# The combine phase in five parts, with all loads of both sums issued in the expert phase into buffers over the first layer's weights

## What is computed

```python
raw_gate = softmax(einsum('btd,de->bte', x, gate))
_, topk_idx = top_k(raw_gate, 3)
mask = one_hot(topk_idx, 16).sum(axis=2)
gate_topk = mask * raw_gate
gate_topk = gate_topk / maximum(sum(abs(gate_topk)), 1e-12)
hidden = relu(einsum('btd,edh->bteh', x, W1) + b1)
expert_out = einsum('bteh,ehd->bted', hidden, W2) + b2
x = layernorm(x + einsum('bte,bted->btd', gate_topk, expert_out))   # eps = 1e-5
```

## Time and profile before

| | us |
|---|---|
| median of 3 runs (lowest, highest) | 1821.72 (1820.7, 1823.14) |
| the profiled execution, own time | 1823.23 |
| its span in the trace | 1821.1 |
| PE busy in the span | 1678.5 (92%) |
| DVE busy | 1392.2 (76%) |
| POOL busy | 1225.5 (67%) |
| ACT busy | 731.6 (40%) |

### The profile page before, as it was taken

The page is one execution under the profiler, slowest core; times in us unless marked ns, Lnnn a source line. Parts: engine busy times, 40 slices in busy tenths (PEclk is TensorE's granted clock), DMA queues, the critical chain, the costliest instruction groups (busy, mean ns, idle before and its releaser), DMA issues. The chain is left out here.

```text
span 1821.1 us, 34011 instructions
## 1 busy us (share of the span) xinstructions
PE 1678.5 (92%) x9489; PEld 1260.4 (69%) x9490; DVE 1392.2 (76%) x3247; ACT 731.6 (40%) x1556; POOL 1225.5 (67%) x1051
## 2 busy tenths in 40 slices
PE   4689999999999999999999999999659999999990
PEld 3566667766666667666676666665339999999980
DVE  3568888888888888998888898887775665656655
ACT  2234454445444444445544444454352222222223
POOL 3257778777887777687876788665017777777764
PEclk9789999999999999999999999999859999999995
DMA  9976456755666777646686565541964444444448
GB/s 308 342 197 174 135 175 201 198 140 163 187 164 179 219 207 203 181 146 183 204 248 178 163 180 166 154 140 50 324 206 70 75 71 71 72 73 74 72 63 282
DMA packets 185395, 302.10 MB, mean 166 GB/s; under 512 B 23616, under 2 KB 82752, under 8 KB 185136
## 3 DMA queue, kind: packets, MB, share of 16 engines
q1 hardware_dynamic: 161888, 269.20, 49.9%
q0 software_dynamic: 21312, 30.02, 10.6%
q10 hardware_dynamic: 2064, 1.31, 0.3%
HBM read 188.67 MB, written 111.54 MB: 165 GB/s over the span
## 5 line engine op out<-in xcount | busy, mean ns | idle before, releaser
L814 ACT ACTIVATE prob<-b_ps 128x512 f32<-128x512 f32 (+3 forms) x768 | 354.6, 489 | 357.2 <-PE b_ps L613 261.1
L540 POOL TENSOR_TENSOR acc<-acc,prob 128x1024 f32<-128x1024 f32 (+1 forms) x188 | 348.3, 1853 | 6.2 <-POOL acc L540 5.2
L612 PE MATMUL b_ps<-q,k 128*128 128x512 f32 (+3 forms) x768 | 294.8, 388 | 4.9 <-ACT prob L814 3.0
L511 POOL TENSOR_TENSOR roped<-rot 128x512 f32<-128x512 f32 x128 | 174.8, 1366 | 166.6 <-DVE rot L959 165.8
L605 PE MATMUL a_ps<-k,q 128*128 128x512 f32 (+3 forms) x768 | 266.1, 383 | 19.7 <-DMA k<-scratch_hilo 9.0
L939 DVE CUSTOM_DVE_ANT_0 masked<-a_ps,causal 128x256 bf16<-128x256 f32 (+3 forms) x512 | 246.1, 496 | 45.3 <-PE a_ps L605 37.8
L695 PE MATMUL y_ps<-prob,v_sb 128*64 128x512 f32 (+3 forms) x1536 | 272.9, 490 | 0.0
L613 PE MATMUL b_ps<-q,k 65*128 65x512 f32 (+3 forms) x768 | 264.4, 348 | 0.0
L1555 POOL DMA_INDIRECT scratch_sum<-y,dst_i x111 | 184.9, 1665 | 96.0 <-ACT y L1627 95.1
L1004 DVE RECIPROCAL inv<-inv 128x128 f32<-128x128 f32 x252 | 229.1, 931 | 2.3
L516 POOL TENSOR_TENSOR lo<-roped,hi 128x512 fp32r<-128x512 f32 x128 | 176.1, 1376 | 81.1 <-ACT hi L827 81.1
(11 more groups left out here) (266 smaller groups left out, 2405.2 us busy)
## 6 DMA issues: line engine op xcount, KB each, us to landing
q<-scratch_hilo SPq DMA_DIRECT2D x192, 256.0 KB, 4.6
k<-scratch_hilo SPq DMA_DIRECT2D x192, 256.0 KB, 5.2
scratch_hilo<-hi SPq DMA_DIRECT2D x64, 512.0 KB, 4.0
scratch_hilo<-lo SPq DMA_DIRECT2D x64, 512.0 KB, 4.7
w_sb<-scratch_wsplit SPq DMA_DIRECT2D x32, 512.0 KB, 3.7
w<-in_L_ffn_W_dram SPq DMA_DIRECT2D x32, 512.0 KB, 9.6
wv_sb<-scratch_wsplit SPq DMA_DIRECT2D x16, 512.0 KB, 7.2
xT<-scratch_xsplit SPq DMA_DIRECT2D x6, 1024.0 KB, 7.6
```

What stands on the lines that cost most here:

```text
L540: nc.gpsimd.tensor_tensor(sums, old, probs(q), ALU.add).then_inc(m["sum_p"], 1)
L612: nc.tensor.matmul(out, k1[s][:, h, js], q1[s][:, h, qs], start=True, stop=False, skip_group_check=True)
L814: nc.scalar.activation(probs(q)[:, h, :], b_ps[:, h, 0:w], ACT.Exp).then_inc(exp_done[h], 1)
```

## The change

1. SP now issues all 16 loads inside the expert phase. Three loads of `sum1` go out when its last scatter has landed (L1542 of the changed kernel), then, behind the landing of the last scatter to `sum0`, the other 13 in turn (L1551, L1552). The combine phase's SP stream has only the stores left.
2. `got0` and `got1` are no longer buffers of the combine phase. They are laid over `w1` (`gathered_sums`), and the combine phase is moved inside the context that holds the weights. Since the loads overwrite `w1`, SP also waits for DVE's last copy out of it.
3. The parts of the layernorm are five: groups 0-1, 2-3, 4-5, 6, 7. DVE now takes the moments of one more group ahead of `finish` in the first three parts, and finishes the last two parts at the end. ACT takes roots 2 and 3 together, and root 4 between the tiles of part 2.
4. The means and variances (`mv`) and the chain's middle value (`near_ps`) lie in PSUM, and no instruction of `finish` has two inputs in SBUF any more; one small copy in each part (L1844) brings the variances to SBUF for ACT. The chain still has six instructions.
5. ACT normalizes 27 tiles, DVE the last 5.

```diff
-PART = 2
-LAST_PART = TILES - LOAD * PART
+PARTS = ((0, 2), (2, 4), (4, 6), (6, 7), (7, 8))
+AHEAD_LOADS = 3
...
+def gathered_sums(S):
+    places = S["w1"][:].rearrange("p e k h -> p (e k h)")
+    got1, got0 = places[:, 0:TILES * D], places[:, TILES * D:TILES * D + 2 * TB * D]
+    return tuple(t.rearrange("p (t d) -> p t d", d=D) for t in (got0, got1))
...
             sums = dram["sum1"].rearrange("(t p) d -> p t d", p=P)
             sp.wait_ge(ys_st[1], scattered(1))
-            sp.dma_start(S["x1b"][:, 0:LOAD, :], sums[:, 0:LOAD, :]).then_inc(S["both_in"][0], 16)
+            for g in range(AHEAD_LOADS):
+                rows = slice(LOAD * g, LOAD * (g + 1))
+                sp.dma_start(S["x1b"][:, rows, :], sums[:, rows, :]).then_inc(S["both_in"][g], 16)
+            sp.wait_ge(m["m_w1"], done(USED_TILES - 1))
+            sp.wait_ge(ys_st[0], scattered(0))
+            got0, got1 = gathered_sums(S)
+            even = dram["sum0"].rearrange("(t p) d -> p t d", p=P)
+            for g in range(LOADS):
+                rows = slice(LOAD * g, LOAD * (g + 1))
+                if g >= AHEAD_LOADS:
+                    place = S["x1b"][:, rows, :] if g < LOADS // 2 else got0[:, LOAD * g - 2 * TB:LOAD * (g + 1) - 2 * TB, :]
+                    sp.dma_start(place, sums[:, rows, :]).then_inc(S["both_in"][g], 16)
+                sp.dma_start(got1[:, rows, :], even[:, rows, :]).then_inc(S["both_in"][g], 16)
...
-        got0 = sb("got0", [P, HALF_TILES, D], F32)
-        got1 = sb("got1", [P, TILES, D], F32)
+        got0, got1 = gathered_sums(S)
...
-        mv = sb("mv2", [P, TILES, 2], F32)
-        r = sb("r2", [P, 5, TILES], F32)
+        small = ctx.enter_context(nc.psum_tensor("small2", [P, 512], F32))
+        mv = small[:, 0:2 * TILES].rearrange("p (t a) -> p t a", a=2)
+        near_ps = small[:, 2 * TILES:3 * TILES]
+        r = sb("r2", [P, 6, TILES], F32)
+        inverse, scales, shifts, _, variance, root_sb = (r[:, i, :] for i in range(6))
+        ACT_TILES = TILES - 5
...
-            for g in range(LOADS):
-                if g:
-                    sp.dma_start(sums_of(g), sums[1][:, rows(g), :]).then_inc(S["both_in"][g], 16)
-                sp.dma_start(got1[:, rows(g), :], sums[0][:, rows(g), :]).then_inc(S["both_in"][g], 16)
...
+            root(0)
+            normalize(0, 0, 8)
+            root(1)
+            normalize(1, 8, 16)
+            root(2)
+            root(3)
+            normalize(2, 16, 20)
+            root(4)
+            normalize(2, 20, 24)
+            normalize(3, 24, ACT_TILES)
...
-                link(V.tensor_tensor(a, first, first, ALU.mult))
-                link(V.scalar_tensor_tensor(out=root, in0=mv[:, tiles_of(h), 1], scalar=EPS, in1=a, op0=ALU.add,
+                link(V.scalar_tensor_tensor(out=near_ps[:, ts], in0=mv[:, ts, 1], scalar=EPS, in1=inverse[:, ts], op0=ALU.add,
                                             op1=ALU.mult))
...
+            moments(0)
+            moments(1)
+            moments(2)
+            finish(0)
+            moments(3)
+            moments(4)
+            finish(1)
+            moments(5)
+            moments(6)
+            finish(2)
+            moments(7)
+            finish(3)
+            finish(4)
...
-        combine_phase(nc, A, dram, S, out)
+            combine_phase(nc, A, dram, S, out)
```

More of the change, by code:

```diff
@@ L1730, in by_act @@
         def by_act(t):
-            return t < LAST_PART or t % 4 == 3
+            return t < ACT_TILES
         def normalized(t, act):
@@ L1739, in tiles_of @@
         def tiles_of(h):
-            return slice(LOAD * PART * h, LOAD * PART * (h + 1))
+            return slice(LOAD * PARTS[h][0], LOAD * PARTS[h][1])
         @block.sync
         def _(sp):
-            sums = [dram[f"sum{i}"].rearrange("(t p) d -> p t d", p=P) for i in range(SUMS)]
-            for g in range(LOADS):
-                if g:
-                    sp.dma_start(sums_of(g), sums[1][:, rows(g), :]).then_inc(S["both_in"][g], 16)
-                sp.dma_start(got1[:, rows(g), :], sums[0][:, rows(g), :]).then_inc(S["both_in"][g], 16)
             for g in range(LOADS):
                 sp.wait_ge(m["c_act"], normalized(LOAD * (g + 1), True))
-                if g >= LOADS - PART:
+                if LOAD * (g + 1) > ACT_TILES:
                     sp.wait_ge(m["c_dve"], normalized(LOAD * (g + 1), False))
@@ L1766, in _, with root, normalize @@
             nc.scalar.activation(r[:, 3, 0:1], eps[:, 0:1], ACT.Sqrt)
-            for h in range(LOADS // PART):
+            def root(h):
                 act.wait_ge(m["c_var"], h + 1)
-                nc.scalar.activation(r[:, 0, tiles_of(h)], mv[:, tiles_of(h), 1], ACT.Sqrt, bias=eps[:, 0:1])\
+                nc.scalar.activation(root_sb[:, tiles_of(h)], variance[:, tiles_of(h)], ACT.Sqrt, bias=eps[:, 0:1])\
                     .then_inc(m["c_std"], 1)
+            def normalize(h, first, end):
                 act.wait_ge(m["c_rs"], h + 1)
[L1772 to L1775, removed]
+                for t in range(first, end):
+                    nc.scalar.activation(got1[:, t, :], sum_of(t), ACT.Identity, bias=shifts[:, t:t + 1],
+                                         scale=scales[:, t:t + 1]).then_inc(m["c_act"], 1)
+            root(0)
[8 more added lines that the diff above has]
+            normalize(3, 24, ACT_TILES)
         @block.vector
@@ L1788, in finish, with moments @@
             def finish(h):
-                root, first, a, rs, shift = (r[:, i, tiles_of(h)] for i in range(5))
+                ts = tiles_of(h)
                 dve.wait_ge(m["c_std"], h + 1)
-                link(V.reciprocal(first, root))
-                link(V.tensor_tensor(a, first, first, ALU.mult))
-                link(V.scalar_tensor_tensor(out=root, in0=mv[:, tiles_of(h), 1], scalar=EPS, in1=a, op0=ALU.add,
+                link(V.reciprocal(inverse[:, ts], root_sb[:, ts]))
+                link(V.scalar_tensor_tensor(out=near_ps[:, ts], in0=mv[:, ts, 1], scalar=EPS, in1=inverse[:, ts], op0=ALU.add,
                                             op1=ALU.mult))
-                link(V.tensor_scalar(a, root, -0.5, 1.5, ALU.mult, ALU.add))
-                link(V.tensor_tensor(rs, first, a, ALU.mult))
-                V.scalar_tensor_tensor(out=shift, in0=mv[:, tiles_of(h), 0], scalar=-1.0, in1=rs, op0=ALU.mult,
+                link(V.tensor_tensor(near_ps[:, ts], near_ps[:, ts], inverse[:, ts], ALU.mult))
+                link(V.tensor_scalar(near_ps[:, ts], near_ps[:, ts], -0.5, 1.5, ALU.mult, ALU.add))
+                link(V.tensor_tensor(scales[:, ts], near_ps[:, ts], inverse[:, ts], ALU.mult))
+                V.scalar_tensor_tensor(out=shifts[:, ts], in0=mv[:, ts, 0], scalar=-1.0, in1=scales[:, ts], op0=ALU.mult,
                                        op1=ALU.mult).then_inc(m["c_rs"], 1)
-            V.memset(eps[:], EPS).then_inc(m["c_eps"], 1)
-            for g in range(LOADS):
+            def moments(g):
                 dve.wait_ge(m["c_added"], g + 1)
@@ L1809, in _ @@
                     ins = V.bn_aggr(mv[:, t, :], stats[:, t, :])
[L1810 to L1817, removed]
+                closed = [h for h, (_, end) in enumerate(PARTS) if end == g + 1]
+                if closed:
+                    link(ins)
+                    V.tensor_copy(variance[:, tiles_of(closed[0])], mv[:, tiles_of(closed[0]), 1]).then_inc(m["c_var"], 1)
+            V.memset(eps[:], EPS).then_inc(m["c_eps"], 1)
+            moments(0)
[11 more added lines that the diff above has]
+            finish(4)
+            dve.wait_ge(m["c_rs"], len(PARTS))
+            for t in range(ACT_TILES, TILES):
+                V.tensor_scalar(got1[:, t, :], sum_of(t), scales[:, t:t + 1], shifts[:, t:t + 1], ALU.mult, ALU.add)\
+                    .then_inc(m["c_dve"], 1)
 def post_ln_block(nc, A, dram, out):
```

## The result

The changed kernel is **slower**, though by little: 1829.60 us (median of 13 runs, 1825.8 to 1836.32) against 1823.14 for the kernel before (median of 13 in the same comparison, 1819.51 to 1827.42). The ratio is 1.0040, with a 95% interval of 1.0031 to 1.0050, all of it above 1. On 1823 us that is +7.3 us; +6.8 was forecast.

The account below looks back on a forecast made before the run. Before, the loads set the adds' pace; changed, the barrier behind SP's issues delays them. 9.6 us later start, 3.4 shorter work, 0.6 more for last stores: +6.8 us, span 1827.9 (1828.5 against the median), range 1824.0 to 1832.5.

Parts of the forecast that it names:

- The barrier: Between expert and combine phase: all engines wait for SP's issues, so POOL's first add moves to 1795.75, 9.6 us later.
- the end of SP's last issue: SP, ahead of the expert block's end: the last of 16 issues ends when load number 10 lands, at 1795.3.
- number 0: First of the loads, numbered 0 to 15 in the new order; it lands at 1781.2 as before, after 4.3 us.
- my 2.9 us: First load on SP: of 4.3 us to land 1.4 is transfer, so some 2.9 us pass before the first data.
- The rule of five: SP's load issues: an issue ends only when the load five before it has landed.
- POOL: Combine phase: eight adds back to back, 2.36 us each plus 0.05 between, end at 1815.0; POOL loses 6.2 us.
- DVE and ACT: Combine phase walk through moments, chains, roots and tiles: 27.6 us from first add to last tile, before 31.0.
- PSUM: DVE's small instructions writing to PSUM: price unknown, taken as 0; the walk could end 1.0 or 2.2 us later.
- The end: Last two stores start at 1823.2 and 1823.6, the second lands at 1827.5, span ends 0.4 us later; 0.6 us more.
- The barrier does not come late: Rival: first add starts at 1785.3, span 1817.5 (-3.6 us) or 1818.1; chance 0.10 together with its 1819.7 variant.
- Part of the delay is made good: Rival: ACT's wait for roots does not hold DVE, end at 1825.4, +4.3 us, or +3.3; chance 0.08.
- The chains still wait for POOL: Rival: adds hold two-input instructions in chains 0 to 2, 2 us each chain, walk ends near 1836, +15 at most; chance 0.05.

Follow-up runs that it names:

- e1: Changed kernel with only five loads issued in the expert phase, the other eleven at the start of the combine phase: 1820.74 us, ratio 0.9981.
- e5_eleven_ahead: Changed kernel with eleven loads issued in the expert phase and five in the combine phase: 1823.60 us in its only run.
- e3: Kernel before with only the loads moved: all sixteen in the expert phase, buffers over the weights, four parts, old chain in SBUF: 1840.58 us, ratio 1.0098.
- e4: Changed kernel with the small tensor (means, variances, chain's middle value) in SBUF in place of PSUM: 1837.17 us, ratio 1.0081.
- e6: Changed kernel with each 512 KB load cut into two of 256 KB, all 32 still in the expert phase: 1828.98 us in its only run.
- e7: Changed kernel with the eight loads of sum0 issued from ACT, SP issuing only sum1, all ahead of the barrier: 1825.47 us in its only run.
- e2: Changed kernel with loads placed as before, one in the expert phase and fifteen in the combine phase: 1820.63 us, ratio 0.9986.

## Why the prediction was right, and where its terms were off

*The barrier* was the term that made the sign, and it is shown: e1 undoes it alone and the first add goes from 20.5 to 9.5 us behind the first issue; e5_eleven_ahead puts it in between. Forecast were 9.6 us of delay for the first add; from the first issue on it is 20.5 - 9.3 = 11.2 us. The term that was too small is the end of SP's last issue. I had it 18.4 us behind the first one, at 1795.3, by letting number 0 land after 4.3 us, seven more at 1.38 each and three at 1.49. It was 20.1 us, at 1796.74. Number 10, issued at 1787.95, landed 8.5 us later, at 1796.45:

```profile
w<-scratch_sum SPq DMA_DIRECT2D x1, 512.0 KB, 8.5
```

So of 1.6 us, 0.8 is number 0 (5.1 us with three loads sent together), 0.5 the ten behind it and 0.3 the time from the landing to the issue's end. A part of it is this one execution: in e3 and e4 the same 16 issues gave the first add at 19.9 and 20.0 us, 10.6 to 10.7 of delay. The rate was lower at first (us; the last two columns are DMA share and GB/s):

```profile
1779.00:1781.00 2.00, 0.00 (x0) 0.00 (x0) 0.00 (x0) 0.00 (x0) 0.00 (x0) 0.50 0.96 295
1781.00:1783.00 2.00, 0.00 (x0) 0.00 (x0) 0.00 (x0) 0.00 (x0) 0.00 (x0) 0.50 1.03 344
1783.00:1785.00 2.00, 0.00 (x0) 0.00 (x0) 0.00 (x0) 0.00 (x0) 0.00 (x0) 0.50 1.08 378
```

Why it is lower was not tried. The Trainium skill's 600 ns to the first byte ("DMA: Bandwidth & Descriptors", "Latency and other measured facts") would have put the first add further off still, and it is not the time that I set it against: my 2.9 us run to the landing. Here the first packet too took longer than that: in the kernel before, SP's queue had begun none 1.2 us after the start of the issue at 1776.86, and seven after 1.5 us.

*The rule of five* was right as to these loads of 512 KB from one engine, and as a rule wrongly put: e6 shows that it is an amount, e7 that each issuing engine has its own and that it is set by what has not begun to move, not by what has not landed. For the forecast that made no difference.

*POOL* needs 2.31 us an add back to back (9.24 / 4), and I had 2.41 with the pause. *DVE and ACT* went as walked through: chain 1 waits 0.63 us for root 1, chain 2 0.43 us. From the first add to the last tile it is 26.8 us for 27.6 forecast. Only 0.3 of these 0.8 us are POOL's, for three adds, since DVE waits for an add the last time here:

```profile
1804.14 1.41 DVE L1837 BATCH_NORM_STATS2 stats<-x1b 128x6 f32<-128x256 f32 x4 [0.27 <-POOL x1b L1779]
```

The rest is in rows that I had added end to end: chain 3 ends at 1821.15 and chain 4 has begun at 1821.07, and roots 2 and 3 take 0.47 us together where I had 0.58. *PSUM* cost nothing: 0.17 us in each instruction, aggregation 0.39 against 0.38.

*The end* took 4.8 us from the last tile, and I had 4.3 to 4.5. The store of group 7 had to follow that of group 6 on SP, was issued 0.4 us behind its last tile and took 4.1 us to land:

```profile
L1772 SPq DMA_DIRECT2D out_dram<-w x1: 509/509/509, 1824.4 to 1824.4; - x1
DMA to landing us min/median/max: 4.1/4.1/4.1
```

Together, in the trace's own time: +1.4 for the last issue, -0.8 from the first add to the last tile and +0.3 at the end give the 0.9 us by which the span (1828.8 for 1827.9) is longer than forecast. That it is no more is in part luck, as the first two have opposite signs.

*The rivals.* "The barrier does not come late" fell with the SP drain at 1796.8. "Part of the delay is made good" fell with its condition: the roots on ACT do hold DVE, 1.1 us in sum. "The chains still wait for POOL" is what e4 makes of the kernel, at 1835.2 for the 1836 that the rival had. That its number is so near is luck: it had 2 us in each of three chains, and in e4 the first chain alone takes 8.5 us more and ends at 1813.55, when the adds are over. The rule of the Trainium skill that speaks against it ("SBUF — State Buffer", "Who interferes with whom") holds here in both halves, with `TENSOR_SCALAR` as the exception that the last section tells of.

*Where the expected gain went.* The three gains of the change are there: data some 2 us earlier (the last load lands 27.4 us behind the first issue for 29.5 before; I had 3.7 us), a chain that is never held, and five parts; the last two were tried only together. Set free of the barrier they give 3.1 us (e1 against before in the table), of which all but the loads' new place gives 1.3 (e2). The version with five loads ahead is faster than both kernels, by 0.2% against the one before, just clear of its interval.

## What to carry over

Issuing a transfer early is free only as long as the issuing engine is not held by it: count what is under way at that point, and look at what that engine must still do, a block's barrier above all. Before a barrier put as many issues as pass at once, and the rest behind it (here five passed at once, and with eight the barrier still opened before the first add's data were there); beyond that an engine that only sends can stop four that compute. And when one engine's work is pressed together, look for instructions of another that had run in its pauses: what was 3.7 us of stalls here became 10 us when the pauses were gone (e3).

## What the runs showed that was not expected

A DVE instruction with a single tensor input is held by a running add on POOL too, if it is a `TENSOR_SCALAR` or a `COPY` from SBUF to SBUF in float32: 2.27 us and 0.44 us above, in place of 0.17. `RECIPROCAL` beside the same adds took 0.17 to 0.20 us, and the moments' instructions kept their times. The Trainium skill has this in the same section of "SBUF — State Buffer": copy, cast and `tensor_scalar` can take DVE's second port. With operand and result in PSUM (L1829 in the change) or the operand alone (L1844) neither is held, 0.17 us each.

The other is that an engine's limit of transfers under way is its own, some 2000 packets not yet begun (e7). Two engines had ten loads of 512 KB under way at once, twice what one had, though each was then held for its own.
